# Attention scores written a second time with keys on partitions, in place of transposing the probabilities (16-head ALiBi attention inside a four-layer kernel, one NeuronCore)

## The chip, the cores and the metric

The kernel runs on one core of one Trainium2 chip (trn2). The metric is the device time of one execution in microseconds; 625.41 us is the median of three runs of the kernel before.

## The reference, cut to what matters

Six stages work on a tensor `x` of 1024 tokens by 256 features: a feed-forward stage `ffn0` (dense and 8 experts), a small attention `attn0`, `ffn0` again, `ffn1` (8 experts), the attention `attn1`, and `ffn1` again. Only `attn1` is changed:

```
x = x + _L1_attn_ref(_layernorm(x), ...)          # on (4, 256, 256)

def _L1_attn_ref(hidden_states, w_dkv, w_q, w_uk, w_uv, w_o):
    HEADS = 16; HEAD_DIM = 16; SLOPE = 0.0625
    def alibi_bias(seq_len):                      # i query, j key
        return where(j <= i, -SLOPE * (i - j), -inf)
    c_kv = hidden_states @ w_dkv.T
    q = (hidden_states @ w_q.T).reshape(B, S, HEADS, HEAD_DIM)
    k = (c_kv @ w_uk.T).reshape(B, S, HEADS, HEAD_DIM)
    v = (c_kv @ w_uv.T).reshape(B, S, HEADS, HEAD_DIM)
    scores = einsum("bqhd,bkhd->bhqk", q, k) * HEAD_DIM ** -0.5
    scores = scores + alibi_bias(S)
    attn = softmax(scores, axis=-1)
    out = einsum("bhqk,bkhd->bqhd", attn, v).reshape(B, S, HIDDEN)
    return out @ w_o.T
```

There are 4 samples of 256 tokens and 16 heads, so 64 heads in all, each with a 256 by 256 causal score matrix.

## The kernel before

It is written engine by engine: each engine's program is one list in the order of the code, and semaphores (`wait_ge`, `then_inc`) join them. Nothing is reordered by a scheduler; the order around the change is that of the loops over `hb` below.

`attn1` handles two blocks of 512 tokens (`b` = 0, 1), each of two samples. A block first projects q, the latent and k (every fp32 product as three matmuls of a high and a low part, `split3`, lines 447 to 449), and builds the stacked operands `qs` and `ks` with two 512-column matmuls for each pair of heads (lines 703 and 704). `qs` and `ks` hold 48 rows for a head: three parts of 16, at partitions 0 to 47 for even heads and 64 to 111 for odd ones. They are of type fp32r, `pb`, `pbt` and `va` are plain fp32.

Then comes the head loop, `for hb in range(2 * HEADS)`, 32 heads for each block:

- TensorE, `scores(hd)` (lines 713 and 715): queries on partitions. 128 columns for the first half of the queries (its keys are the first 128), 256 for the second half. The causal quarter that is all masked is never computed. It writes one of three banks.
- VectorE, `bias_min(hd)` (line 1471): adds `bias` (ALiBi and mask) to the negated scores in PSUM and takes each row's minimum into `nmin`, one instruction for 128 columns and one for 256.
- ScalarE, lines 989 and 991: the exponential with `nmin` as its per-partition bias, into `pb`.
- TensorE, `probs_turn(hd - 3)` (line 723): three 128 by 128 transposes of `pb` into another bank, since the next product needs the keys on partitions.
- ScalarE for heads 1 and 3 of four (line 1011) and VectorE for 0 and 2 (line 1479), `probs_t`: copy the result to `pbt`.
- TensorE, `pv` (line 737): for a group of four heads, probabilities times values, with a column of ones in `va` that gives the sum of the row. Its two halves `c` stand in two neighbouring iterations. ScalarE copies the group's result out (`out_t`).
- `out_back`, `out_turn` and `out_project` (lines 754, 761 and 447 to 449) finish a sample's output; they stand at fixed iterations of the loop. `transposes` (line 457) turns the next block's normalised input.

`ffn0` and `ffn1` are long streams of 128-row, 256- and 512-column matmuls.

Of the kernel before, what the change touches and what calls it, by code (L numbers as in the profile page):

```python
# [48 lines left out]
STEP = 64  # L49

# [7 lines left out]
def program(nc, x_in, w0, w1, wr, pre, posts, att0, r0, ident_in, cap_in, iota_in, wa, sel_in, bias_in, out,  # L58
            stages=STAGES):
    with ExitStack() as ctx:  # L60
# [80 lines left out]
        sel = sb("sel", [P, 4, 4, P], F32R)  # L141
        bias = sb("bias", [P, 3 * P])
# [8 lines left out]
        pb = sb("pb", [P, 4, 3 * P])  # L151
        pbt = sb("pbt", [P, 2, 4, 3 * P])

        wa_raw = va[:, :, :, :].rearrange("p t h s -> p (t h s)")[:, 0:WA]
        sel_raw = pbt[:, :, :, :].rearrange("p g j q -> p (g j q)")[:, 0:16 * P]
# [6 lines left out]
        nmin = sb("nmin", [P, 4, 2])  # L162
# [85 lines left out]
        sm_s = sem("scores_biased")  # L248
        exp_s = sem("probs_ready")
        t_ps = sem("probs_t_in_psum")  # L250
        ptd_s = sem("probs_t_by_dve")
        pta_s = sem("probs_t_by_act")
# [47 lines left out]
        by_act = (1, 3)  # L300

        def copied(hd):

            mine = [j for j in range(4) if (j in by_act) == (hd % 4 in by_act)]
            return pta_s if hd % 4 in by_act else ptd_s, len(mine) * (hd // 4) + mine.index(hd % 4) + 1

        def pv_bank(g):

            return 2 if g % 8 == 7 else 5

        def score_bank(hd):
            return hd % (2 * HEADS) % 3

        def turn_bank(hd):
            return (3, 4, 6)[hd % 3]
# [35 lines left out]
        def _(pool):  # L351
# [74 lines left out]
            for st in plan:  # L426
# [10 lines left out]
                if st.kind == "ffn1" and st.k == 0 and "attn1" in stages:  # L437
                    pool.wait_ge(wal_s, WL)
                    nc.gpsimd.memset(va[:, :, :, :], 0.0).then_inc(wal_s, 1)
                    pool.wait_ge(wal_s, WL + 1)  # L440
                    nc.gpsimd.memset(va[:, :, :, HD:HD + 1], 1.0).then_inc(wal_s, 1)


        @block.tensor
        def _(pe):
# [156 lines left out]
            def attn1(st):  # L602
                p = st.p
                for b in range(2):
# [42 lines left out]
                    for hb in range(2 * HEADS):  # L647
                        hd = 2 * HEADS * b + hb
                        if hb == 0:
                            continue  # L650
                        if hb < HEADS:
                            s = HEADS // 2 + hb // 2
                            pe.wait_ge(std_s if s % 2 else sta_s, 8 * b + s // 2 + 1)
                        if hb < 3:
                            pe.wait_ge((sta_s, std_s)[hb - 1], 8 * b + 7)
                        scores(hd)
# [8 lines left out]
                        for i, (at, step) in enumerate(zip((7, 9, 12, 14), 2 * (out_back, out_turn, out_project))):  # L665
                            if hb == HEADS + at:
                                step(2 * b, i // 3)
                    probs_turn(2 * HEADS * (b + 1) - 3)
                    out_turn(2 * b, 1)
                    probs_turn(2 * HEADS * (b + 1) - 2)  # L670
                    for c in range(2):
                        pv(8 * (b + 1) - 2, c)
                    probs_turn(2 * HEADS * (b + 1) - 1)
                    if b == 0 or st.after:

                        transposes(p + b + 1)
                    out_project(2 * b, 1)
                    for c in range(2):
                        pv(8 * (b + 1) - 1, c)
# [27 lines left out]
            def scores(hd):  # L707
# [3 lines left out]
                if hd >= 3:  # L711
                    pe.wait_ge(exp_s, hd - 2)
# [5 lines left out]
            def probs_turn(hd):  # L718
                pe.wait_ge(exp_s, hd + 1)
                if hd >= 3:  # L720
                    pe.wait_ge(*copied(hd - 3))
                for c in range(3):
# [341 lines left out]
        def _(dve):  # L1064
# [325 lines left out]
            def attn1(st):  # L1390
                p = st.p
                for b in range(2):
# [37 lines left out]
                    for hb in range(2 * HEADS):  # L1430
# [7 lines left out]
                        if hb:  # L1438
                            bias_min(hd)
# [193 lines left out]
```

## Time and profile before

| | |
|---|---|
| median of three runs | 625.41 us (622.27 to 628.8) |
| profiled execution: its span | 628.7 us; the page gives the execution no other time, and the highest run was 628.8 |
| TensorE matmul busy | 584.4 us, 93% of the span |
| TensorE weight load busy | 467.3 us, 74% |
| VectorE, ScalarE, GpSimd busy | 433.0, 270.5 and 82.9 us |
| mean granted TensorE clock | 0.883 |

Busy shares are of the whole span. A matmul's end is modelled in the trace, so a matmul is busy longer than the engine needs for it; the distance between the starts of two neighbours tells what one costs. The clock is a share of full speed (2.4 GHz): 1.00 or 0.50, and a mean between them where it changed inside a stretch.

### The profile page before, as it was taken

The page shows a single profiled execution, that of the slowest core. Times are in us where ns is not written, and L with a number is a line of the kernel's source. Part 1 is how long each engine was busy: PE and PEld are TensorE (multiplying, and loading weights), DVE is VectorE, ACT ScalarE, POOL GpSimd, SP SyncE. Part 2 cuts the span into 40 slices and gives each one's busy share as a digit, 9 for nine tenths or more (in the row PEclk, how much of TensorE's full clock was granted, in tenths as well). Part 3 has the DMA queues.
Part 4 walks back from the last instruction along what each step waited for, and adds up shares of the span by engine and source line. Part 5 has one row for each costly group of instructions (what it writes and reads, how often), then busy time and mean ns, then how long its engine had stood idle before and what let it go on. Part 6 is the DMA issues. An engine that isn't in the chain of part 4 may idle for free.

```text
span 628.7 us, 9327 instructions
## 1 busy us (share of the span) xinstructions
PE 584.4 (93%) x3170; PEld 467.3 (74%) x3170; DVE 433.0 (69%) x1251; ACT 270.5 (43%) x603; POOL 82.9 (13%) x94
## 2 busy tenths in 40 slices
PE   2999999999689999999999589899999999999995
PEld 1788888888568888888888578765566855568885
DVE  4667985887853457648778899786454784546986
ACT  3557434632212253245426235264543465443341
POOL 1001000010110000000103536300000000003442
PEclk9999999999869999999999799895556965559998
DMA  5322202000000000000000030000000000000001
GB/s 174 103 93 82 84 19 66 18 2 0 1 1 1 0 1 2 2 0 1 2 0 2 0 139 1 1 1 2 1 1 1 0 2 2 0 1 2 2 33 34
DMA packets 7102, 13.75 MB, mean 22 GB/s; under 512 B 1296, under 2 KB 3600, under 8 KB 6928
## 3 DMA queue, kind: packets, MB, share of 16 engines
q1 hardware_dynamic: 6000, 12.65, 6.3%
q10 hardware_dynamic: 1056, 0.51, 0.3%
q8 instruction: 26, 0.43, 0.3%
q14 instruction: 20, 0.16, 0.1%
HBM read 12.11 MB, written 1.05 MB: 21 GB/s over the span
## 4 chain that ended last, share of the span: by engine, by line
PE 81%; DVE 11%; issue 3%; ACT 2%; POOL 1%; DMA 1%; ACTq 1%; DVEq 0%; POOLq 0%
PE ps L447 19%; PE ps L449 18%; PE ps L448 18%; PE ps L723 8%; PE ps L737 4%; PE ps L713 4%; PE ps L715 3%; DVE gel L1203 3%; PE ps L457 1%; PE ps L703 1%; DVE z L1125 1%; DVE gel L1201 1%; PE ps L704 1%; PE ps L754 1%; DMA post_b<-in_posts_dram 1%
## 5 line engine op out<-in xcount | busy, mean ns | idle before, releaser
L447 PE MATMUL ps<-zh,w0u_h 128*128 128x512 f32 x256 | 102.8, 402 | 2.5 <-issue 2.5
L449 PE MATMUL ps<-zl,w0u_h 128*128 128x512 f32 x256 | 102.2, 399 | 0.0
L448 PE MATMUL ps<-zh,w0u_l 128*128 128x512 f32 x256 | 101.8, 398 | 0.0
L870 ACT ACTIVATE gel<-ps 128x512 f32<-128x512 f32 x64 | 38.2, 597 | 105.5 <-PE ps L449 105.3
L1221 DVE TENSOR_TENSOR act<-gel,ps 128x512 f32<-128x512 f32 x64 | 43.8, 685 | 53.5 <-ACT gel L870 53.4
L447 PE MATMUL ps<-w0d_h,ah 128*128 128x256 f32 x256 | 73.3, 286 | 1.2 <-DVE al L1228 1.0
L448 PE MATMUL ps<-w0d_h,al 128*128 128x256 f32 x256 | 72.4, 283 | 0.0
L449 PE MATMUL ps<-w0d_l,ah 128*128 128x256 f32 x256 | 72.4, 283 | 0.0
L1471 DVE CUSTOM_DVE_ANT_0 ps<-ps,bias 128x128 f32<-128x128 f32 (+1 forms) x128 | 43.2, 383 | 41.0 <-PE ps L715 40.8
L1228 DVE TENSOR_TENSOR al<-act,ah 128x512 fp32r<-128x512 f32 x64 | 43.9, 687 | 23.5 <-ACT ah L876 23.2
L407 POOL TENSOR_TENSOR al<-act,ah 128x512 fp32r<-128x512 f32 x32 | 42.1, 1316 | 137.1 <-ACT ah L944 136.7
L876 ACT ACTIVATE ah<-act 128x512 fp32r<-128x512 f32 x64 | 40.3, 630 | 41.5 <-DVE act L1221 41.5
L447 PEld LDWEIGHTS ps<-zh,w0u_h 128*128 128x128 f32 x256 | 49.0, 191 | 12.1 <-issue 2.9
L449 PEld LDWEIGHTS ps<-zl,w0u_h 128*128 128x128 f32 x256 | 48.8, 191 | 11.8
L448 PEld LDWEIGHTS ps<-zh,w0u_l 128*128 128x128 f32 x256 | 49.0, 192 | 9.3
L723 PE MATMUL ps<-ident,pb 128*128 128x128 f32 x192 | 54.3, 418 | 0.0
L447 PEld LDWEIGHTS ps<-w0d_h,ah 128*128 128x128 f32 x256 | 48.8, 191 | 4.4 <-issue 2.2
L1203 DVE SCALAR_TENSOR_TENSOR gel<-ps,aff,gel 128x256 f32<-128x256 f32 x112 | 46.3, 475 | 7.3 <-PE ps L449 5.9
L448 PEld LDWEIGHTS ps<-w0d_h,al 128*128 128x128 f32 x256 | 48.9, 191 | 2.3
L449 PEld LDWEIGHTS ps<-w0d_l,ah 128*128 128x128 f32 x256 | 49.0, 192 | 0.0
L447 PE MATMUL ps<-w_h,ah 128*128 128x256 f32 x128 | 37.9, 296 | 11.6 <-DVE gel L1201 7.4
L1203 DVE SCALAR_TENSOR_TENSOR macc<-ps,aff,macc 128x256 f32<-128x256 f32 x112 | 46.3, 476 | 0.7 <-PE ps L449 0.2
(180 smaller groups left out, 1156.1 us busy)
## 6 DMA issues: line engine op xcount, KB each, us to landing
stage<-in_w_dram SPq DMA_DIRECT2D x16, 384.0 KB, 3.0
stage<-in_w_dram SPq DMA_DIRECT2D x8, 256.0 KB, 2.6
x<-in_x_dram SPq DMA_DIRECT2D x2, 512.0 KB, 5.1
pbt<-in_sel_dram SPq DMA_DIRECT2D x1, 1024.0 KB, 6.6
out_dram<-x SPq DMA_DIRECT2D x2, 512.0 KB, 2.9
va<-in_wa_dram SPq DMA_DIRECT2D x1, 896.0 KB, 5.1
post_b<-in_posts_dram ACTq DMA_DIRECT2D x1, 388.0 KB, 5.6
bias<-in_bias_dram SPq DMA_DIRECT2D x1, 192.0 KB, 7.2
```

The lines of the kernel that those rows point to most:

```text
L407: nc.gpsimd.tensor_tensor(al[:, slot, :], act32[:, n % 2, :], ah[:, slot, :].bitcast(F32), ALU.subtract).then_inc(al1_s, 1)
L447: pe.matmul(o, lh, rh, start=start, stop=False, **kw)
L448: pe.matmul(o, ll, rh, start=False, stop=False, **kw)
L449: return pe.matmul(o, lh, rl, start=False, stop=stop, **kw)
L713: pe.matmul(ps[:, score_bank(hd), 0:P], qs[r0:r1, h // 2, t0:t0 + P], ks[r0:r1, h // 2, t0:t0 + P], start=True, stop=True)
L723: mm = pe.transpose(ps[:, turn_bank(hd), c * P:(c + 1) * P], pb[:, hd % 4, c * P:(c + 1) * P], ident[:, :])
L870: nc.scalar.activation(gel[:, n % 2, :], ps[:, 2 * (n % 2), :], ACT.Gelu_apprx_tanh).then_inc(gelu_s, 1)
L876: nc.scalar.activation(ah[:, n % NA, :], act32[:, n % 2, :], ACT.Copy).then_inc(ah_s, 1)
L1203: i = V.scalar_tensor_tensor(sums[:, t, :], o, a, sums[:, t, :], ALU.mult, ALU.add)
L1221: V.tensor_tensor(act32[:, n % 2, :], gel[:, n % 2, :], ps[:, 2 * (n % 2) + 1, :], ALU.mult)\
L1228: V.tensor_tensor(al[:, n % NA, :], act32[:, n % 2, :], ah[:, n % NA, :].bitcast(F32), ALU.subtract)\
L1471: i = V.tensor_tensor_reduce(s, s, bias[:, lo:hi], 1.0, FAR, ALU.add, ALU.min, nmin[:, hd % 4, c:c + 1])
```

## The change

The scores are computed twice. The first time (queries on partitions) they serve only for the row minimum. The minima of four heads are then split into a high and a low part and written, with constants, as columns of the tile `shift`; TensorE transposes `shift` once for four heads (`shift_turn`) and ScalarE copies it to `shift_t`. The second time (`scores_t`, keys on partitions) four matmuls add into one bank: the row minimum and the ALiBi term from `shift_t` (33 rows, 384 columns), the scores of the two halves (48 rows, 128 and 256 columns), and the causal mask (128 rows, 256 columns). The exponential reads that bank and writes `pbt` at once, so `pb`, the transposes of probabilities and the copies to `pbt` are gone. `scores_t` runs 6 iterations behind `scores`, and the loop has 12 iterations more (`SUM`) in which no new head starts. `bias` now lies in `tmp` and `shift` in `macc`; the constants `sel` grow by half.

```diff
-        sel = sb("sel", [P, 4, 4, P], F32R)
+        sel = sb("sel", [P, 6, 4, P], F32R)
...
         def score_bank(hd):
-            return hd % (2 * HEADS) % 3
-        def turn_bank(hd):
-            return (3, 4, 6)[hd % 3]
+            return hd % 2
+        def turned_bank(hd):
+            return 3 + hd % 2
...
# TensorE, head loop
-                    for hb in range(2 * HEADS):
+                    for hb in range(2 * HEADS + SUM):
...
-                        scores(hd)
...
-                        if hb >= 3:
-                            probs_turn(hd - 3)
-                        if hb % 4 in (1, 2) and hb >= 8:
-                            pv(hd // 4 - 2, hb % 4 - 1)
...
+                        if 0 < hb < 2 * HEADS:
+                            scores(hd)
...
+                        if hb % GROUP == 1 and GROUP < hb < 2 * HEADS + GROUP:
+                            shift_turn(hd // GROUP - 1)
+                        if TURN <= hb < 2 * HEADS + TURN:
+                            scores_t(hd - TURN)
+                        if hb % GROUP == 0 and hb >= SUM:
+                            for c in range(2):
+                                pv((hd - SUM) // GROUP, c)
...
-            def probs_turn(hd):
-                pe.wait_ge(exp_s, hd + 1)
-                if hd >= 3:
-                    pe.wait_ge(*copied(hd - 3))
-                for c in range(3):
-                    mm = pe.transpose(ps[:, turn_bank(hd), c * P:(c + 1) * P], pb[:, hd % 4, c * P:(c + 1) * P],
-                                      ident[:, :])
-                mm.then_inc(t_ps, 1)
+            def shift_turn(g):
+                if g == 0:
+                    pe.wait_ge(shz_s, 2)
+                pe.wait_ge(shl_s, g + 1)
+                if g:
+                    pe.wait_ge(sht_s, g)
+                for i, block in enumerate((3, 0, 2)):
+                    mm = pe.transpose(ps[:, 2, i * P:(i + 1) * P], shift[:, g % 2, block, :], ident[:, :])
+                mm.then_inc(sht_ps, 1)
+
+            def scores_t(hd):
...
+                pe.wait_ge(sht_s, hd // GROUP + 1)
+                if hd >= 2:
+                    pe.wait_ge(exp_s, hd - 1)
+                pe.matmul(ps[:, bank, 0:3 * P], sel[r0:r0 + LATE_ROW + 1, 4, hd % GROUP, :],
+                          shift_t[r0:r0 + LATE_ROW + 1, hd // GROUP % 2, :], start=True, stop=False,
+                          skip_group_check=True)
+                pe.matmul(ps[:, bank, 0:P], ks[r0:r1, h // 2, t0 + P:t0 + 2 * P], qs[r0:r1, h // 2, t0 + P:t0 + 2 * P],
+                          start=False, stop=False, skip_group_check=True)
+                pe.matmul(ps[:, bank, P:3 * P], ks[r0:r1, h // 2, t0:t0 + P], qs[r0:r1, h // 2, t0:t0 + 2 * P],
+                          start=False, stop=False, skip_group_check=True)
+                pe.matmul(ps[:, bank, 0:2 * P], sel[:, 5, 0, :], sel[:, 5, 1:3, :].rearrange("p c q -> p (c q)"),
+                          start=False, stop=True, skip_group_check=True).then_inc(t_ps, 1)
...
# ScalarE
-                        nc.scalar.activation(pb[:, hd % 4, 0:P], ps[:, score_bank(hd), 0:P], ACT.Exp,
-                                             bias=nmin[:, hd % 4, 0:1], scale=-1.0)
-                        nc.scalar.activation(pb[:, hd % 4, P:3 * P], ps[:, score_bank(hd), P:3 * P], ACT.Exp,
-                                             bias=nmin[:, hd % 4, 1:2], scale=-1.0).then_inc(exp_s, 1)
...
+            def shift_out(g):
+                act.wait_ge(sht_ps, g + 1)
+                if g >= 2:
+                    act.wait_ge(t_ps, GROUP * (g - 1))
+                nc.scalar.activation(shift_t[:, g % 2, :], ps[:, 2, 0:3 * P], ACT.Copy).then_inc(sht_s, 1)
...
-                nc.scalar.activation(pbt[:, hd // 4 % 2, hd % 4, :], ps[:, turn_bank(hd), 0:3 * P], ACT.Copy)\
-                  .then_inc(pta_s, 1)
+                nc.scalar.activation(pbt[:, hd // GROUP % 2, hd % GROUP, :], ps[:, turned_bank(hd), 0:3 * P], ACT.Exp,
+                                     scale=-1.0).then_inc(exp_s, 1)
...
# VectorE
-            def probs_t(hd):
...
-                V.tensor_copy(pbt[:, hd // 4 % 2, hd % 4, :], ps[:, turn_bank(hd), 0:3 * P]).then_inc(ptd_s, 1)
+            def shift_hi(g):
...
+                V.tensor_copy(hi.bitcast(F32R), m).then_inc(shh_s, 1)
+
+            def shift_lo(g):
+                m, hi, lo = shifts(g)
+                dve.wait_ge(shh_s, g + 1)
+                V.tensor_tensor(lo, m, hi, ALU.subtract).then_inc(shl_s, 1)
```

TensorE before, in the middle of the head loop of the first block: `L713` and `L715` are the scores of one head, `L723` the transposes of the head three before it, `L737` half of a group's product with the values (its stationary operand has 32 columns; shapes are stationary columns by moving columns).

```order
L713 MATMUL ps<-ks,qs 128x128
L715 MATMUL ps<-ks,qs 128x256
L723 MATMUL ps<-ident,pb 128x128 x3
L737 MATMUL ps<-pbt,va 32x256 x4
L713 MATMUL ps<-ks,qs 128x128
L715 MATMUL ps<-ks,qs 128x256
L723 MATMUL ps<-ident,pb 128x128 x3
L737 MATMUL ps<-pbt,va 32x128 x4
```

TensorE in the changed kernel at the same place, with its own line numbers: `L715` and `L717` are the scores, `L738` to `L745` the four matmuls of `scores_t`, `L757` the product with the values, `L727` the transposes of `shift`.

```order
L715 MATMUL ps<-ks,qs 128x128
L717 MATMUL ps<-ks,qs 128x256
L738 MATMUL ps<-shift_t,sel 128x384
L741 MATMUL ps<-qs,ks 128x128
L743 MATMUL ps<-qs,ks 128x256
L745 MATMUL ps<-sel 128x256
L757 MATMUL ps<-pbt,va 32x256 x4
L757 MATMUL ps<-pbt,va 32x128 x4
L715 MATMUL ps<-ks,qs 128x128
L717 MATMUL ps<-ks,qs 128x256
L727 MATMUL ps<-ident,macc 128x128 x3
L738 MATMUL ps<-shift_t,sel 128x384
```

Three transposes of each head gave way to four matmuls of each head, three transposes stand once in four heads, and the two halves of the product with the values now follow each other.

ScalarE before, in the same loop: two exponentials for each head and, for every second one, the copy of line 1011.

```order
L989 ACTIVATE pb<-ps,nmin 128x128
L991 ACTIVATE pb<-ps,nmin 128x256
L1011 ACTIVATE pbt<-ps 128x384
L989 ACTIVATE pb<-ps,nmin 128x128
L991 ACTIVATE pb<-ps,nmin 128x256
```

ScalarE in the changed kernel: `L1028` is the exponential of a head, `L1022` the copy to `shift_t`, `L1035` the copy of a group's output.

```order
L1028 ACTIVATE pbt<-ps 128x384 x3
L1022 ACTIVATE shift_t<-ps 128x384
L1028 ACTIVATE pbt<-ps 128x384
L1035 ACTIVATE gel<-ps 128x256
L1028 ACTIVATE pbt<-ps 128x384 x3
```

One instruction of 384 columns for a head took the place of two exponentials and half a copy.

## Rows read from the trace of the kernel before

**Rows 1.** The page's chain of work that ended last, its shares by line

```profile
PE ps L447 19%; PE ps L449 18%; PE ps L448 18%; PE ps L723 8%; PE ps L737 4%; PE ps L713 4%; PE ps L715 3%; DVE gel L1203 3%; PE ps L457 1%; PE ps L703 1%; DVE z L1125 1%; DVE gel L1201 1%; PE ps L704 1%; PE ps L754 1%; DMA post_b<-in_posts_dram 1%
```

**Rows 2.** Windows: busy of PE, PEld, DVE, ACT, POOL, clock, DMA

```profile
410.00:416.00 6.00, 6.00 (x32) 4.86 (x31) 5.72 (x12) 3.98 (x7) 0.00 (x0) 1.00 0.01 3
422.00:428.00 6.00, 6.00 (x23) 3.87 (x23) 5.43 (x29) 3.65 (x11) 0.61 (x2) 0.58 0.00 0
464.00:470.00 6.00, 6.00 (x29) 4.10 (x28) 3.37 (x15) 3.28 (x9) 0.00 (x0) 0.50 0.00 0
476.00:482.00 6.00, 6.00 (x40) 4.47 (x40) 2.38 (x8) 1.92 (x5) 0.00 (x0) 0.58 0.00 0
482.00:488.00 6.00, 4.96 (x43) 3.95 (x43) 3.31 (x8) 2.37 (x7) 0.00 (x0) 1.00 0.01 3
```

**Rows 3.** Timeline of PE, four heads (start, busy, line, shapes)

```profile
442.24 0.47 PE L713 MATMUL ps<-ks,qs 48*128 48x128 f32 x1
442.51 0.52 PE L715 MATMUL ps<-ks,qs 48*128 48x256 f32 x1
442.96 0.90 PE L723 MATMUL ps<-ident,pb 128*128 128x128 f32 x3
443.79 0.47 PE L713 MATMUL ps<-ks,qs 48*128 48x128 f32 x1
...
445.35 1.08 PE L737 MATMUL ps<-pbt,va 128*32 128x256 f32 x8
446.36 0.47 PE L713 MATMUL ps<-ks,qs 48*128 48x128 f32 x1
...
447.91 0.66 PE L737 MATMUL ps<-pbt,va 128*32 128x128 f32 x8
448.50 0.47 PE L713 MATMUL ps<-ks,qs 48*128 48x128 f32 x1
...
450.05 0.47 PE L713 MATMUL ps<-ks,qs 48*128 48x128 f32 x1
```

**Rows 4.** Timeline of PE, one head of the second block, before the clock fell

```profile
506.35 0.33 PE L713 MATMUL ps<-ks,qs 48*128 48x128 f32 x1
...
506.77 0.55 PE L723 MATMUL ps<-ident,pb 128*128 128x128 f32 x3
507.25 0.32 PE L713 MATMUL ps<-ks,qs 48*128 48x128 f32 x1
```

**Rows 5.** Timeline of PE, the end of an output projection inside the loop

```profile
469.43 0.41 PE L448 MATMUL ps<-wa_h,otl 128*128 128x256 f32 x1
469.64 0.41 PE L449 MATMUL ps<-wa_l,oth 128*128 128x256 f32 x1
469.99 0.47 PE L713 MATMUL ps<-ks,qs 48*128 48x128 f32 x1
```

**Rows 6.** Timeline of PE, both halves of a group's product with the values

```profile
479.00 1.50 PE L737 MATMUL ps<-pbt,va 128*32 128x256 f32 x16
480.44 0.79 PE L723 MATMUL ps<-ident,pb 128*128 128x128 f32 x3
```

**Rows 7.** Timeline of DVE, the start of one head's minimum and of the next

```profile
420.45 0.33 DVE L1471 CUSTOM_DVE_ANT_0 ps<-ps,bias 128x128 f32<-128x128 f32 x1
...
421.08 0.33 DVE L1471 CUSTOM_DVE_ANT_0 ps<-ps,bias 128x128 f32<-128x128 f32 x1
```

**Rows 8.** Groups of ACT, 428 to 476 us (busy, mean ns, idle before)

```profile
L991 ACT ACTIVATE pb<-ps,nmin 128x256 f32<-128x256 f32 x24 | 11.2, 467 | 0.0
L989 ACT ACTIVATE pb<-ps,nmin 128x128 f32<-128x128 f32 x24 | 8.8, 368 | 24.0 <-DVE nmin L1471 24.0
L1011 ACT ACTIVATE pbt<-ps 128x384 f32<-128x384 f32 x12 | 5.9, 488 | 0.0
L1018 ACT ACTIVATE gel<-ps 128x256 f32<-128x256 f32 x4 | 1.5, 384 | 0.0
```

**Rows 9.** Timeline of PE, head 6 of the first block

```profile
423.51 0.47 PE L713 MATMUL ps<-ks,qs 48*128 48x128 f32 x1
```

**Rows 10.** Timeline of PE, the last output transposes, the second block's first matmul

```profile
484.87 1.09 PE L754 MATMUL ps<-ident,act 128*128 128x128 f32 x8 [0.50 <-ACT act L1018]
485.72 0.48 PE L447 MATMUL ps<-zh,wa_h 128*128 128x512 f32 x1
```

More of the change, by code:

```diff
@@ L49 @@
 STEP = 64
+GROUP = 4
+ONE_ROW, LATE_ROW = 2 * GROUP, 32
+TURN = 6
+SUM = 12
+OUT_STEPS = (27, 29, 32, 34, 36, 38)
 Stage = namedtuple("Stage", "s kind p k before after d0 d1")
@@ L140, in program @@
         wa_l = sb("wa_l", [P, WA], F32R)
-        sel = sb("sel", [P, 4, 4, P], F32R)
-        bias = sb("bias", [P, 3 * P])
+        sel = sb("sel", [P, 6, 4, P], F32R)
+        bias = tmp[:, :, :].rearrange("p t d -> p (t d)")[:, 0:3 * P]
         ch = sb("ch", [P, BLK], F32R)
@@ L298, in program @@
         TK = 11
[L300 to L305, printed above, removed]
         def pv_bank(g):
-            return 2 if g % 8 == 7 else 5
+            return 6 if g % 8 == 7 else 5
         def score_bank(hd):
-            return hd % (2 * HEADS) % 3
-        def turn_bank(hd):
-            return (3, 4, 6)[hd % 3]
+            return hd % 2
+        def turned_bank(hd):
+            return 3 + hd % 2
         def out_bank(n, t):
@@ L441, in _ @@
                     nc.gpsimd.memset(va[:, :, :, HD:HD + 1], 1.0).then_inc(wal_s, 1)
+                    nc.gpsimd.memset(shift[:, :, :, :], 0.0).then_inc(shz_s, 1)
+                    pool.wait_ge(shz_s, 1)
+                    for r in range(2):
+                        c = STEP * r
+                        nc.gpsimd.memset(shift[:, :, :, c + ONE_ROW:c + ONE_ROW + 1], 1.0)
+                        i = nc.gpsimd.memset(shift[:, :, 3, c + LATE_ROW:c + LATE_ROW + 1], 1.0)
+                    i.then_inc(shz_s, 1)
         @block.tensor
@@ L660, in attn1 @@
                             pe.wait_ge(v_s, b + 1)
-                        if hb >= 3:
-                            probs_turn(hd - 3)
-                        if hb % 4 in (1, 2) and hb >= 8:
-                            pv(hd // 4 - 2, hb % 4 - 1)
[L665 to L679, printed above, removed]
+                        if hb % GROUP == 1 and GROUP < hb < 2 * HEADS + GROUP:
[5 more added lines that the diff above has]
+                                pv((hd - SUM) // GROUP, c)
+                        if hb in OUT_STEPS:
+                            i = OUT_STEPS.index(hb)
+                            (out_back, out_turn, out_project)[i % 3](2 * b, i // 3)
+                        if hb == 2 * HEADS + 1 and (b == 0 or st.after):
+                            pe.wait_ge(sm_s, 2 * HEADS * (b + 1))
+                            transposes(p + b + 1)
                 if st.after != "ffn1":
@@ L730, in pv @@
                 if c == 0:
-                    for j in (2, 3):
-                        pe.wait_ge(*copied(4 * g + j))
+                    pe.wait_ge(exp_s, GROUP * (g + 1))
                     if g and pv_bank(g) == 5:
@@ L1615 @@
                         sel[(2 * pair + e) * HD + r, kind, pair, STEP * e + HD * part + r] = 1.0
+    for r in (0, STEP):
+        for j in range(GROUP):
+            sel[r + j, 4, j, :] = sel[r + GROUP + j, 4, j, :] = -1.0
+            sel[r + ONE_ROW, 4, j, :] = -0.0625 * np.arange(P)
+            sel[r + LATE_ROW, 4, j, :] = -0.0625 * P
+    sel[:, 5, 0, :] = np.eye(P)
+    sel[:, 5, 1, :] = sel[:, 5, 2, :] = np.where(np.arange(P)[:, None] > np.arange(P)[None, :], FAR, 0.0)
     q, j = np.arange(SEQ)[:, None], np.arange(SEQ)[None, :]
-    far = np.where(j <= q, 0.0625 * (q - j), FAR).astype(np.float32)
+    far = np.where(j <= q, -0.0625 * j, FAR).astype(np.float32)
     bias = np.concatenate([far[:P, :P], far[P:, :]], axis=1)
```

117 lines of the change are left out of this document (62 added, 55 removed).

## The prediction

> **What bounds the kernel now.** I read first the page's chain of work that ended last. It lies almost wholly on TensorE, most of it in the feed-forward streams (lines 447 to 449), which the change leaves alone; the head loop of the attention (lines 723, 737, 713 and 715) makes up 19% of the span [rows 1]. So the question is what the change does to TensorE's time in the two head loops, and little else.
>
> Then I read the windows. In the head loop TensorE is busy 6.00 of every 6 us, VectorE and ScalarE about half of that [rows 2]: the loop is bound by TensorE alone. The same rows show that the granted clock is 1.00 (2.4 GHz) while 512-column matmuls on 128 rows run, mixes both levels in the window from 422 us, is 0.50 (1.2 GHz) at 464, and comes back inside 476 to 482. The reader is to see that a TensorE that is busy all the time runs most of this loop at half speed. Two things set the time of this change: how much the engine has to stream and to switch, and at which of the two clocks.
>
> Third, the timeline gives the cost of each piece, from start to start, at 1.2 GHz [rows 3]. Scores of a head: 442.24 to 442.96, 0.72 us. Three transposes: 442.96 to 443.79, 0.83 us. Together 1.55 us for a head. The product with the values adds 446.36 - 445.35 = 1.01 us for one half and 448.50 - 447.91 = 0.59 us for the other, and a group of four heads takes 450.05 - 442.24 = 7.81 us. At 2.4 GHz the scores take 0.42 us and the transposes 0.48 [rows 4].
>
> **Prices for the new pieces.** Inside a run of 256-column matmuls on 128 rows, 469.43 to 469.64 gives 0.21 us, or 0.83 ns a column [rows 5]. The 384 columns of scores are then 0.32 us of streaming, and 0.72 - 0.32 = 0.40 us goes to changing to 48 rows and back out of them. Three transposes at the same 0.21 us are 0.64, and 0.19 us is switching. One such pair of switches costs 0.59 us at 1.2 GHz. That is the largest hidden cost here, as the new order keeps the switches: the scores and the first three matmuls of scores_t run on 48 or 33 rows, then the mask matmul runs on 128 rows, and then the next head begins.
>
> **Part by part, at 1.2 GHz.**
>
> - Removed: three transposes for each head, 0.64 us of streaming. Their 0.19 us of switching, and the 0.40 us of the scores, are inherited by the mask matmul and by the run ahead of it.
> - Added: scores_t, 384 + 128 + 256 + 256 = 1024 columns, 0.85 us of streaming, and a pair of switches. No row shows fp32r matmuls going from 48 to 128 rows. The cheapest row is 128 to 48 rows, 469.64 to 469.99, 0.35 us for a matmul of 0.21, so 0.14 for a change and 0.28 for two [rows 5]. The dearest reading is that every short matmul on few rows pays what line 713 pays, 0.27 us for 0.11 of streaming, 0.16 more, three times over in scores_t: 0.59 + 0.48 = 1.07. I take 0.53, next to the 0.59 which the same places cost now and a little under it, since the mask matmul loads fp32r, not fp32. scores_t is 1.38 us.
> - Added: shift_turn once in four heads. It breaks the run of few-row matmuls in two, so it costs a full transposing part and one more entry: 0.83 + 0.40 = 1.23 us.
> - Moved: the two halves of the product with the values now stand together; where they do so already, they take 480.44 - 479.00 = 1.44 us [rows 6] against 1.01 + 0.59 = 1.60. This gives back 0.16 us a group.
> - ScalarE: one exponential of 384 columns. Between 128 and 256 columns it grows by 0.10 us, so 0.57, and with a quarter of a 0.49 us copy and of a 0.38 us copy 0.79 us a head [rows 8]. VectorE: its minimum takes 0.63 us a head as now [rows 7], and two small instructions for four heads stand in place of two copies. Both engines stay well under TensorE's head, so I cost what they save at nothing; TensorE's own work covers it.
> - New waits: scores_t waits for the exponential of the head two before it, because of its bank, and scores for the minimum two before. Each has one whole head of TensorE's work, over 1.5 us, against 0.57 and 0.63. shift_turn stands 2 iterations behind the minimum that it needs, the first use of shift_t one iteration behind shift_turn. Covered in the loop; behind shift_turn everything of TensorE is queued, but it would wait only in the first group, where TensorE has little else to do.
> - The larger constants, the clearing of shift and the moved bias lie beside the feed-forward streams: nothing.
>
> **The sum for one block.** In the kernel before, head 6 starts at 423.51 [rows 9] and the next block's first matmul at 485.72 [rows 10]: 62.2 us. My prices reproduce this: 26 heads' scores at 0.32 (8.3), 29 heads of transposes and switches at 1.23 (35.7), products with the values 12.0, output steps 24 matmuls and transposes at 0.21 (5.1), waits 1.0, sum 62.1.
>
> For the changed kernel the scores of the first six heads come at VectorE's pace, 0.63 us each, so scores_t of head 0 begins at about the same 423.5. From there: 32 scores_t at 1.38 (44.2), 25 heads' scores at 0.32 (8.0), 7 shift_turn at 1.23 (8.6), 8 products at 1.44 (11.5), output steps 5.1, the next block's 8 transposes 1.3, waits 1.0: 79.7 us. That is 17.5 us more a block, 35 for both. Against the profiled execution's 628.7 us this is 664; against the median of 625.4, which lies 3.3 lower, **660 us**.
>
> The bounds of scores_t's switching move this: 0.28 in place of 0.53 takes 0.25 x 64 = 16 us off (644), 1.07 adds 0.54 x 64 = 35 us (695). I think the low one nearer, since the second matmul of a run may load its weights behind the one before it.
>
> **Which clock.** The whole sum rests on 1.2 GHz. For it: before the fall at the loop's entry the engine ran scores on 48 rows and a few transposes with waits between them, and the new loop starts thinner still, with nothing but scores at VectorE's pace and three transposes. While the clock is low, the loop before gets through six 256-column matmuls of an output projection on 128 rows, and the clock is still 0.50 in that window [rows 2, 5]. The new loop alternates short matmuls on 48 and 33 rows, one on 128 rows and about a third of the time in switches. It is denser than the old one, but far from the streams that run at 1.00.
>
> **The rivals.**
>
> - The clock comes up and stays up (2.4 GHz through both loops). For it: transposes go, real matmuls take their place, and the clock is the one thing which could change by a factor of two. The price, all with halved streaming: scores_t 0.425 + 0.26 + 0.16 = 0.85 us (the switches from the 0.42 and 0.48 us of [rows 4]), times 32 is 27.0; scores 25 x 0.16 = 4.0; shift_turn 7 x 0.74 = 5.2; products 8 x 0.72 = 5.8; the rest 4.4; 46.4 us a block against 62.2, 32 us less for both: 593 us. This is the case on the other side; it decides when over half of each loop runs at 2.4 GHz, since a block gains 16 us at one clock and loses 17.5 at the other. Against it: the entry, as above. The clock did rise inside 476 to 482, where the engine ran almost only transposes and products with the values, and was 1.00 in the next window [rows 2], so a loop of transposes is not what alone holds it down. I give 10%.
> - The Trainium skill's page "TensorE: Matmul & The Clock Gate", in "Part 4: PE-mode transpose", says that the full clock doesn't engage for transposes, as these don't count as TensorE being busy in the same way; by that rule taking out transposes for matmuls would free the clock, and the time would be that of this first rival. The trace speaks against it at 476 to 482.
> - The clock comes up for part of the loops, about half: gain and loss cancel, about 624 us. 6%.
> - The few-row matmuls hide no load at all, or the wait for shift_t shows in each group: above 684 us. 3%.
>
> **How the numbers follow.** The forecast, low clock and prices within the bounds, has 81%. Its range, 640 to 684 us, takes in the lower bound and two thirds of the way to the upper one; the rest, the two cases of a higher clock and the heavy tail, is 19% and left out. About 1%, 6 us, is what a measurement of this kernel can tell from no change. Faster by more: the first rival and some of the second, 14%. Within 1%: 4%. Slower: 82%.
>
> **What would show it.** In the profile after: the granted clock of the windows from 425 to 495 us, 0.50 by the forecast and 1.00 by the rival; the distance from one head's scores to the next, 1.7 us (four heads with their group's work 9.5 against 7.81), or 1.0 at 2.4 GHz; TensorE's idle time in the loops still near nothing, with ScalarE at under half; the feed-forward stages unchanged to a microsecond. I am wrong if the clock is high, wrong in size if the mask matmul's switches differ from 0.53 us, and wrong in kind if TensorE waits for ScalarE or VectorE in the middle of the loop.

## The result and the profile after

The changed kernel takes 688.8 us (median of 4 runs, 685.2 to 692.5), the kernel before 627.0 us (622.3 to 628.8) in the same job: 1.104 times as long, 95% interval 1.094 to 1.113. I had forecast 660 us with a range up to 684. The sign and the mechanism came out, the size didn't: +60.3 us between the profiled spans (689.0 against 628.7), where my working gave +35. A few executions keep or lose the full clock over a whole loop (of the kernel before, two took 598.6 and 598.9 us at a mean clock of 0.947 and two 699.9 and 702.5 us at 0.71, the others 618.6 to 631.0 at 0.88 to 0.91), so where the runs of an experiment split like this, each kind is given.

The first view is again the page, with its slices of the granted clock and its chain of work that ended last.

```profile
PEclk9999999998599999999989997555559555557998
...
PE ps L456 18%; PE ps L458 17%; PE ps L457 17%; PE ps L745 5%; PE ps L738 4%; PE ps L757 3%; PE ps L715 3%; PE ps L743 3%; PE ps L717 3%; DVE gel L1220 2%; PE ps L727 2%; PE ps L466 2%; PE ps L705 1%; PE ps L774 1%; DVE z L1142 1%
```

The chain is the one of [rows 1] with the head loop's lines exchanged: 745, 738, 757, 715, 743, 717 and 727 make up 23% of 689 us, where 723, 737, 713 and 715 made up 19% of 629. The two long stretches of 5 in the clock's line are the head loops. In the samples of the clock they last 92.2 us from 421.8 and 95.6 us from 534.5; before, 58.0 from 423.0 and 54.6 from 508.3. So the level in the loops, 0.50, is as forecast, and the slow stretches grew by 34 and 41 us.

The windows (columns as in [rows 2]), in the middle of the loop, at its end and where the next block begins:

```profile
464.00:470.00 6.00, 6.00 (x25) 4.27 (x27) 2.60 (x14) 1.62 (x4) 0.00 (x0) 0.50 0.00 0
506.00:512.00 6.00, 4.22 (x26) 2.59 (x25) 1.93 (x4) 1.07 (x4) 0.00 (x0) 0.50 0.00 0
512.00:518.00 6.00, 5.59 (x28) 4.70 (x29) 2.84 (x8) 1.97 (x5) 0.00 (x0) 0.83 0.00 0
```

In the middle TensorE (second column) has work in all of the 6 us, VectorE in 2.60 and ScalarE in 1.62: the loop is still bound by TensorE alone. What is new against [rows 2] stands at the end: before, the clock came up inside 476 to 482, ahead of the loop's tail; now it stays at 0.50 to the end of the tail and comes up at 514.0, as the next block's streams begin (after the second block at 630.1, 2.8 us into them).

The timeline of TensorE, one head in the middle of the loop, its successor's first row, and a head before which `shift_turn` stands; it answers to [rows 3]:

```profile
442.31 0.47 PE L715 MATMUL ps<-ks,qs 48*128 48x128 f32 x1
442.58 0.52 PE L717 MATMUL ps<-ks,qs 48*128 48x256 f32 x1
442.90 0.52 PE L738 MATMUL ps<-shift_t,sel 33*128 33x384 f32 x1
443.22 0.30 PE L741 MATMUL ps<-qs,ks 48*128 48x128 f32 x1
443.33 0.52 PE L743 MATMUL ps<-qs,ks 48*128 48x256 f32 x1
443.77 0.58 PE L745 MATMUL ps<-sel 128*128 128x256 f32 x1
444.29 0.47 PE L715 MATMUL ps<-ks,qs 48*128 48x128 f32 x1
...
449.95 0.52 PE L717 MATMUL ps<-ks,qs 48*128 48x256 f32 x1
450.41 0.90 PE L727 MATMUL ps<-ident,macc 128*128 128x128 f32 x3
...
453.07 0.52 PE L717 MATMUL ps<-ks,qs 48*128 48x256 f32 x1
```

A head takes 444.29 - 442.31 = **1.98 us**, against 1.55 before and a forecast of 1.70. The price of each matmul is the distance between its start and the next one's, less the streaming at 0.83 ns a column. Line 738, 384 columns, takes 443.22 - 442.90 = 0.32 us: all streaming. Line 741, 0.11 us: all streaming. But 743 to 745, where the rows go from 48 to 128, is 0.44 us for 0.21 of streaming; 745 to the next head's 715, back to 48 rows, 0.52 for 0.21 (0.31 more); 715 itself takes 0.27 for 0.11, and 717 takes 0.32 for 0.21. Of the 1.98 us, 1408 columns stream for 1.17, and 0.81 us is switching, where I had allowed 0.53. The kernel before has 0.59 of it in the same places [rows 3]: its way out of the 48 rows (0.45 for 0.21) and its first load (0.27 for 0.11) cost what they cost here, its way back behind three transposes only 0.19, and it has no third load in the run, the one that costs 0.11 here.

The weight loads (PEld) of the same head show why the dear places are the ones after a change:

```profile
442.30 0.28 PEld L715 LDWEIGHTS ps<-ks,qs 48*128 48x128 f32 x1 [0.22 <-issue]
442.47 0.33 PEld L717 LDWEIGHTS ps<-ks,qs 48*128 48x128 f32 x1
442.69 0.33 PEld L738 LDWEIGHTS ps<-shift_t,sel 33*128 33x128 f32 x1
442.90 0.33 PEld L741 LDWEIGHTS ps<-qs,ks 48*128 48x128 f32 x1
443.22 0.33 PEld L743 LDWEIGHTS ps<-qs,ks 48*128 48x128 f32 x1
443.77 0.29 PEld L745 LDWEIGHTS ps<-sel 128*128 128x128 f32 x1 [0.22 <-issue]
```

Four loads follow each other at about 0.2 us from 442.30, no faster, and the short matmuls at the start of the run go at their pace; from line 741 on the load starts a whole matmul ahead of its own (442.90 for 443.22). At 443.77 and 442.30 the load engine stood still for 0.22 us and the load starts together with its matmul. Such a load isn't hidden behind an earlier matmul.

The end of the block, which answers to [rows 5] and [rows 10]. The rows at 500.37 and 501.93 are the starts of two `scores_t` with no new scores between them, 1.56 us apart:

```profile
495.75 0.58 PE L745 MATMUL ps<-sel 128*128 128x256 f32 x1
496.13 1.91 PE L466 MATMUL ps<-ident,z 128*128 128x128 f32 x8
...
500.37 0.69 PE L738 MATMUL ps<-shift_t,sel 33*128 33x384 f32 x1
...
501.93 0.69 PE L738 MATMUL ps<-shift_t,sel 33*128 33x384 f32 x1
...
508.84 0.55 PE L456 MATMUL ps<-wa_h,oth 128*128 128x256 f32 x1 [1.68 <-DVE otl L1526]
...
512.40 1.84 PE L774 MATMUL ps<-ident,act 128*128 128x128 f32 x8 [0.50 <-ACT act L1035]
514.01 0.48 PE L456 MATMUL ps<-zh,wa_h 128*128 128x512 f32 x1
```

The groups of ScalarE in the loop, 428 to 488 us (busy, mean ns, idle before), against [rows 8]:

```profile
L1028 ACT ACTIVATE pbt<-ps 128x384 f32<-128x384 f32 x23 | 11.3, 491 | 31.6 <-PE ps L745 31.6
L1022 ACT ACTIVATE shift_t<-ps 128x384 fp32r<-128x384 f32 x6 | 2.9, 491 | 13.6 <-PE ps L727 13.6
```

Both of ScalarE's groups wait for TensorE, 45.2 of 60 us. The exponential of 384 columns takes 0.49 us, less than the 0.57 I had estimated, and that changes nothing.

### The profile page after: what moved, and what is told of

It is laid out like the page before. It is cut to its first block, busy times and chain, and to the rows that moved or that the text cites. A ratio compares the mean times of both kernels' runs of the same rounds, so it can differ in the third digit from the quotient of the medians.

```text
span 689.0 us, 9401 instructions
## 1 busy us (share of the span) xinstructions
PE 640.9 (93%) x3282; PEld 519.3 (75%) x3282; DVE 425.2 (62%) x1251; ACT 251.0 (36%) x523; POOL 84.1 (12%) x99
## 4 chain that ended last, share of the span: by engine, by line
PE 83%; DVE 10%; issue 3%; ACT 1%; POOL 1%; DMA 1%; ACTq 1%; DVEq 0%; POOLq 0%
PE ps L456 18%; PE ps L458 17%; PE ps L457 17%; PE ps L745 5%; PE ps L738 4%; PE ps L757 3%; PE ps L715 3%; PE ps L743 3%; PE ps L717 3%; DVE gel L1220 2%; PE ps L727 2%; PE ps L466 2%; PE ps L705 1%; PE ps L774 1%; DVE z L1142 1%
## 5 line engine op out<-in xcount | busy, mean ns | idle before, releaser
L1488 DVE CUSTOM_DVE_ANT_0 ps<-ps,tmp 128x128 f32<-128x128 f32 (+1 forms) x128 | 43.3, 383 | 82.1 <-PE ps L717 82.0
L1028 ACT ACTIVATE pbt<-ps 128x384 f32<-128x384 f32 x64 | 31.4, 491 | 91.5 <-PE ps L745 91.5
```

Of the source, the lines that this page charges most:

```text
L1028: nc.scalar.activation(pbt[:, hd // GROUP % 2, hd % GROUP, :], ps[:, turned_bank(hd), 0:3 * P], ACT.Exp, scale=-1.0).then_inc(exp_s, 1)
L1488: i = V.tensor_tensor_reduce(s, s, bias[:, lo:hi], 1.0, FAR, ALU.add, ALU.min, nmin[:, hd // GROUP % 2, c, hd % GROUP:hd % GROUP + 1])
```

## The experiments

Three questions were open: is the extra time the price of changing rows (theory A in the expectations), would the new loop be cheap at the full clock and could it be brought there (theory C), and is it a load's place in the run or the step from 48 to 33 rows that costs 0.11 us at line 717. Each edit is made to the changed kernel, unless the kernel before is named. "Filler" is a matmul whose result nothing uses: it writes a score bank that the scores then overwrite.

Whole times compare these kernels only roughly, since the clock changes its level at different places near the ends of their loops. In the profiled executions, from a block's first `scores_t` to the next stage's first matmul, it is 1.00 for none of the changed kernel's 90.8 + 90.8 us, for 0.1 us without the mask matmul, but for 14.4 us with the mask on 48 rows, 8.9 with the mask on VectorE and 11.7 with the masks in pairs. At 0.50 such a stretch would last up to twice as long. So I also give the time of a group of four heads in the middle of the first loop, where all of them run at 0.50: 10.49 us in the changed kernel.

### The mask matmul on the head's own 48 rows

```diff
-                pe.matmul(ps[:, bank, 0:2 * P], sel[:, 5, 0, :], sel[:, 5, 1:3, :]...
+                pe.matmul(ps[:, bank, 0:2 * P], sel[r0:r1, 5, 0, :], sel[r0:r1, 5, 1:3, :]...
```

> The changed kernel with the mask matmul (256 columns) on the same 48 rows as the scores, in place of 128 rows; the mask is then complete for 48 of 128 keys only. Columns are the same, the change between 48 and 128 rows goes from each head. Theory A (the loss is largely the cost of changing between 48 and 128 rows, at 1.2 GHz): a head falls from 1.98 us to about 1.5, 64 heads give back 27 to 32 us, about 658 us. Rival B (it is the added columns alone): nothing moves, 687 to 690 us. The clock stays at 0.50 in either.

Measured 637.3 us (636.4 to 637.8), 1.018 of the kernel before (1.010 to 1.026), 51.5 us less than the changed kernel with the same columns streamed. Up to 14 us of that can be the clock at the ends of the loops. In the middle, at 0.50, a group falls from 10.49 to 6.87 us, 0.90 us a head, more than the 0.54 of switching on the two sides of the mask matmul, and more than all 0.81 of a head. The timeline of TensorE shows where the rest comes from:

```profile
441.19 0.52 PE L717 MATMUL ps<-ks,qs 48*128 48x256 f32 x1
...
442.47 0.69 PE L738 MATMUL ps<-shift_t,sel 33*128 33x384 f32 x1
442.49 0.47 PE L715 MATMUL ps<-ks,qs 48*128 48x128 f32 x1
442.76 0.52 PE L717 MATMUL ps<-ks,qs 48*128 48x256 f32 x1
442.96 0.30 PE L741 MATMUL ps<-qs,ks 48*128 48x128 f32 x1
443.07 0.52 PE L743 MATMUL ps<-qs,ks 48*128 48x256 f32 x1
...
448.06 0.52 PE L717 MATMUL ps<-ks,qs 48*128 48x256 f32 x1
```

Line 738 starts at 442.47 and the next head's 715 at 442.49, though 738 alone streams for 0.32 us. An even head lies on rows 0 to 47, an odd one on 64 to 111, and matmuls of the two run beside each other. The second head even runs ahead of the program: in TensorE's list its 715 and 717 stand behind the first head's 741 and 743, and they start before these. A group of four heads takes 448.06 - 441.19 = 6.87 us from line 717 to line 717, where the changed kernel takes 453.07 - 442.58 = 10.49 and the kernel before 7.81. The one matmul on 128 rows for each head costs its two changes, and besides it fences the heads off from one another. (A group now costs less than in the kernel before, and the kernel is still slower: the two stretches from the first `scores_t` to the next stage take 60.9 and 66.3 us, those of the kernel before, from head 6 on, 62.2 and 61.0. What the middle gains goes to the longer end of the loop.)

### No mask matmul

Its three lines are left out (and the matmul before it ends the accumulation). The mask is then missing, and the exponential's scale is -0.01, so that values stay finite.

> The changed kernel without the mask matmul: the causal mask is left out of the second scores, and the exponential takes them times 0.01 so that nothing overflows. Theory A: the head loses 0.21 us of streaming and its changes of rows, 1.98 to about 1.25 us, 64 heads give back 45 us, about 643 us. Rival B (columns alone): 0.21 x 64 = 14 us back, 675 us.

Measured 632.6 us (628.6 to 636.8), 1.011 (1.001 to 1.021), 56.2 us back with the clock at 0.50 to the end of both loops. Streaming the mask's columns accounts for 64 x 0.21 = 14 us of it at most, so 42 us or more are its rows. In the middle of the loop, from one group's product with the values to the next, it is 447.07 - 440.62 = 6.45 us, 0.42 less than with the mask on 48 rows, though 4 x 0.21 us of columns are gone. Against the 3.6 us a group that moving it to 48 rows gave, what costs is the rows of that matmul, hardly its columns.

### The mask added by VectorE

```diff
-                pe.matmul(ps[:, bank, 0:2 * P], sel[:, 5, 0, :], sel[:, 5, 1:3, :]...
...
+            def mask_add(hd):
+                dve.wait_ge(t_ps, hd + 1)
+                s = ps[:, turned_bank(hd), 0:2 * P]
+                V.tensor_tensor(s, s, sel[:, 5, 1:3, :].rearrange("p c q -> p (c q)").bitcast(F32), ALU.add).then_inc(msk_s, 1)
```

The exponential waits for `msk_s` in place of `t_ps`.

> The changed kernel with the causal mask added by VectorE into the bank of the second scores ahead of the exponential, in place of the mask matmul; all of the reference is computed. Theory A (TensorE's changes to 128 rows and back were the price): TensorE as in the run without the mask, VectorE takes 0.45 us more for a head beside it, 632 to 640 us. Rival E (VectorE's step in the chain becomes the wait): TensorE idles in the loop, 650 us or more.

Measured 639.0 us (636.4 to 641.8): 49.8 us back (up to 9 of them the clock at the loops' ends), with all of the computation kept, as theory A wanted. A group takes 447.21 - 439.99 = 7.22 us. TensorE now waits now and then for the longer chain behind it:

```profile
445.24 0.65 PE L739 MATMUL ps<-shift_t,sel 33*128 33x384 f32 x1 [0.49 <-ACT pbt L1027]
```

VectorE's addition of 256 columns takes 0.44 us a head; in the window 440 to 446 TensorE is busy for 5.51 us at clock 0.50. Even so this version is some 13 us behind the kernel before.

### The masks of two heads together

```diff
+                            if hb % 2:
+                                mask(hd - TURN - 1)
+                                mask(hd - TURN)
...
-                pe.matmul(ps[:, bank, 0:3 * P], sel[r0:r0 + LATE_ROW + 1, 4, hd % GROUP, :],
+                pe.matmul(ps[:, bank, 0:3 * P], sel[r0:r1, 4, hd % GROUP, :],
```

This halves the changes of rows and keeps every column on TensorE; the product with the values moves one head back. The shift's matmul takes 48 rows in place of 33 too.

> The changed kernel in another order, all of the reference computed: the few-row matmuls of two heads run first and then their two mask matmuls one after the other, the product with the values stands behind them, and the first matmul of the second scores reads 48 rows in place of 33 (the added ones are zero). Theory A (each change to 128 rows and back costs 0.70 us at 1.2 GHz beyond streaming): half of the changes go, 0.35 us or more for each head, 22 to 32 us, 657 to 667 us; more if neighbouring heads, on other rows of the array, run beside each other as they did in the run with the 48-row mask. Theory A2 (the 0.11 us that the 33-row matmul waits for behind the 48-row one is due to the change of rows): that distance falls from 0.32 to 0.21 us. Rival B (columns alone): 687 us.

Measured 656.3 us (653.9 to 661.5), 1.052 (1.044 to 1.061): 32.5 us back, at the upper end of theory A's 22 to 32, which it let grow if heads ran beside each other; up to 12 of it can be the clock at the loops' ends. A group takes 444.74 - 436.68 = 8.06 us. The other half of the edit changes nothing:

```profile
440.60 0.47 PE L718 MATMUL ps<-ks,qs 48*128 48x128 f32 x1
440.87 0.52 PE L720 MATMUL ps<-ks,qs 48*128 48x256 f32 x1
441.13 0.47 PE L718 MATMUL ps<-ks,qs 48*128 48x128 f32 x1
441.19 0.59 PE L741 MATMUL ps<-shift_t,sel 48*128 48x384 f32 x1
```

From line 720 to 741 it is 0.32 us, as from 717 to 738 in the changed kernel, with 48 rows in place of 33. That speaks against the step from 48 to 33 rows as what costs 0.11 us there, and for the place in the run, the third load after a change. It isn't a clean test, as a matmul on the other rows now starts in between (718 at 441.13).

### Fillers in the changed kernel

```diff
+                pe.matmul(ps[:, score_bank(hd), :], wa_h[:, 0:P], wa_h[:, 0:4 * P], start=True, stop=True)
```

One filler of 512 columns on 128 rows ahead of each head's scores. The question is the rival of the full clock.

> The changed kernel with one extra 512-column matmul on 128 rows ahead of each head's first scores, into the bank that these then overwrite; its result is not used. Theory C (the clock at 1.2 GHz holds this loop back, and denser work on 128 rows keeps it at 2.4): clock 1.00 in most of the loops, a head about 1.3 us, 30 us less for each block, 615 to 635 us. Rival D (the clock doesn't answer to such work here): 0.43 us more for each head, 715 to 722 us.

Measured 707.5 us (704.8 to 711.7), 1.132 (1.123 to 1.142), with the clock at 0.50 in both loops. A head takes 445.82 - 443.41 = 2.41 us, 0.43 more. Theory C failed, and the rival was right that in the loop the filler is only added; the whole is 8 us under its 715 to 722. Next, four fillers for each of heads 1 to 5 and one for each later head:

> The changed kernel with the 128-row filler, four of them for each of heads 1 to 5 of a block, where nothing but scores runs, and one for each later head. Theory C (the clock was lost in the thin stretch at the entry, and the filled loop would hold 2.4 GHz if it came in with it): clock 1.00 through both loops, a head about 1.3 us, a block 54 us against 62 before, 605 to 620 us. Rival D (this loop can't hold the clock even so): clock 0.50, 708 to 715 us.

Measured 704.1 us (695.7 to 707.3), within 4 us of the run before and over 80 us above theory C. The clock held through the entry, until 433.6 us, and fell there, where one filler a head was left: 0.97 in the window 428 to 434, 0.50 in 440 to 446. Then two fillers for each later head, and two in each of a block's last six `scores_t`:

> The changed kernel with two 128-row fillers for each head (four for heads 1 to 5 of a block), and two for each of the last six heads' second scores. Theory C: enough to hold 1.00 through both loops; a head with its fillers takes about 1.6 us, 0.46 to 0.5 us of it the fillers, so both blocks together 35 to 50 us less than the changed kernel, 640 to 655 us. Without the fillers a head would take 1.1 us at this clock. Rival D: the clock still falls, 0.86 us more for each head, 740 us.

Measured 684.2 us (three runs 683.1 to 685.5, one 655.8 with a mean clock of 0.969). The profiled execution has both levels, the first block's loop at one and the second's at the other:

```profile
440.00:500.00 60.00, 60.00 (x217) 38.94 (x217) 14.59 (x78) 11.39 (x25) 0.00 (x0) 0.50 0.00 1
548.00:612.00 64.00, 64.00 (x389) 42.94 (x387) 28.83 (x152) 20.31 (x45) 1.20 (x2) 1.00 0.01 1
```

```profile
560.11 0.33 PE L717 MATMUL ps<-ks,qs 48*128 48x128 f32 x1
...
561.17 0.63 PE L716 MATMUL ps<-wa_h 128*128 128x512 f32 x2
561.73 0.32 PE L717 MATMUL ps<-ks,qs 48*128 48x128 f32 x1
```

The timeline shows a head of the second block. With two fillers it takes 561.73 - 560.11 = 1.62 us; less the fillers' 1024 columns, 0.43 us at 2.4 GHz, that leaves 1.19 us. (The same working at 0.50 in this run, 448.93 - 446.10 = 2.83 less 0.85, gives 1.98, the head of the changed kernel.) The kernel before takes 0.90 at that clock [rows 4], so the new form gives TensorE more to do at either clock. My rival of 593 us had 0.85 + 0.16 = 1.01 us in its place: its price was 0.18 us a head too low, and its condition didn't come. Both expectations of this run missed: the three runs at 683 to 685 us have the mean clock of the profiled one, 0.92 to 0.93, with one block high and one low.

The last of them is the version with the mask on VectorE, with four fillers at the entry, two or one later:

> The version with the mask added by VectorE, with fillers on 128 rows: four for heads 1 to 5 of a block, two for two heads of each group of four, one for the others, two for each of the last six heads' second scores. All of the reference is computed. Theory C: clock 1.00 in both loops, then VectorE (1.1 us a head) and TensorE (1.1 to 1.3) are about level, 590 to 610 us, faster than both kernels. Rival: the clock falls, 670 us.

Measured 707.3 us (704.5 to 708.7), 1.132 (1.124 to 1.140), with the clock at 0.50 for 75.1 us from 427.8 and for 81.9 from 547.2. The expectation failed by a hundred microseconds. Fillers that don't hold the clock are only columns, and beside that they fence the heads off again.

### Fillers in the kernel before

The same line of 512 columns, put ahead of the scores in the kernel before:

> The kernel before with the same extra 512-column matmul ahead of each head's scores, result not used. Theory C: clock 1.00 in the head loops, a head about 1.15 us in place of 1.55, 15 us less for each block, about 595 us, faster than both kernels. Rival D: clock stays 0.50, 0.43 us more for each head, about 655 us.

Measured **598.7 us** (596.3 to 601.5), 0.958 of the kernel before (0.949 to 0.966). The window in the middle of the loop has the clock at 1.00, and so has the whole attention; [rows 2] have 0.50 at 464:

```profile
440.00:446.00 6.00, 6.00 (x45) 3.71 (x44) 3.91 (x20) 3.96 (x11) 0.00 (x0) 1.00 0.00 0
```

```profile
440.11 0.32 PE L714 MATMUL ps<-ks,qs 48*128 48x128 f32 x1
...
440.53 0.55 PE L724 MATMUL ps<-ident,pb 128*128 128x128 f32 x3
440.83 0.47 PE L713 MATMUL ps<-wa_h 128*128 128x512 f32 x1
441.24 0.32 PE L714 MATMUL ps<-ks,qs 48*128 48x128 f32 x1
```

A head with its filler takes 441.24 - 440.11 = 1.13 us, where without it and at 0.50 it was 1.55 [rows 3]. All the transposes are still there. The same 512 columns on the head's 48 rows (`wa_h[r0:r1, 0:P], wa_h[r0:r1, 0:4 * P]`):

> The kernel before with the same 512-column filler for each head, but on the 48 rows of the head's own scores in place of 128; result not used. It streams the same columns and changes rows no more often than without it. Theory C1 (the clock follows how long the array streams, whatever the rows): clock 1.00 as with the 128-row filler, 596 to 602 us. Theory C2 (rows in use count too): the clock falls at the loop's entry and stays at 0.50 in the loops, 0.43 us more for each head than before, 650 to 660 us.

Three runs at 650.6 to 654.7 us and one at 626.0 (mean clock 0.918, against 0.87), and in the profiled one the clock is at 0.50 in both loops:

```profile
440.00:446.00 6.00, 6.00 (x26) 3.99 (x26) 2.51 (x11) 3.29 (x9) 0.00 (x0) 0.50 0.00 0
```

TensorE is as busy by the profile in both, with the same columns. On 128 rows they held the clock in all four executions, on 48 rows in three of four they didn't. With 256 columns on 128 rows:

> The kernel before with a filler of 256 columns in place of 512, on 128 rows. Theory C: still enough to hold the clock at 1.00, 0.10 us less for each head than the 512-column filler, about 592 us. Rival: too thin, the clock falls to 0.50 in the loops and the filler costs 0.21 us a head on top of the kernel before, about 640 us.

Measured 616.1 us (613.1 to 622.9), between the two: in the profiled execution the first loop is at 0.50 (68.3 us of it), the second at 1.00 from end to end. Last, 512 columns for the first eight heads of a block and 256 for the others:

> The kernel before with the 128-row filler of 512 columns for the first eight heads of a block and of 256 columns for the other 24, results not used. The kernel with 256 columns everywhere lost the clock at the entry of one block and held it at 1.00 through the whole other one. Theory F (the entry decides, and 256 columns hold the clock once the loop runs): clock 1.00 in both blocks in every execution, 0.10 us less for each of 48 heads than with 512 columns, 592 to 595 us. Rival G (the loop with 256 columns also loses it in the middle): a block at 0.50 costs about 24 us, 610 to 620 us.

Five runs at 592.2 to 596.1 us, one at 627.3 with a mean clock of 0.912. In the profiled execution the clock is 1.00 in both loops, and a head takes 431.45 - 430.43 = 1.02 us:

```profile
430.43 0.32 PE L715 MATMUL ps<-ks,qs 48*128 48x128 f32 x1
...
431.45 0.32 PE L715 MATMUL ps<-ks,qs 48*128 48x128 f32 x1
```

That is 30 us less than the 626.2 of the kernel before in that job, for most executions, and the fastest version here; the form with 512 columns throughout is the steadier of the two in these few runs.

## Why the prediction was wrong in size

- **The bound and the clock: right.** TensorE is busy for 6.00 of 6 us in the loop at 0.50, ScalarE and VectorE wait for it. That TensorE would wait for ScalarE or VectorE in the middle of the loop didn't happen.
- **The step that failed is the term "I take 0.53" for the switching of `scores_t`.** Stretches of nothing but `scores_t` have 1.56 us a head (500.37 to 501.93) where I had 1.38, so the term is 0.71. I had started from 0.59, what the same places cost in the kernel before, and gone a little under it because the mask matmul loads fp32r. No run shows anything to take off for that. And one of the places got dearer: the way out to 128 rows costs 0.23 and the first load 0.17, as before, but the way back from the one mask matmul costs 0.30, where behind three transposes it cost 0.19. Of this 0.30, 0.17 is paid too where transposes on 128 rows come next (495.75 to 496.13, 0.38 us for 0.21), so it belongs to the mask matmul's standing alone and not to the rows behind it. The rest is the 0.14 us of my lower bound [rows 5], the way back to 48 rows when a long stream on 128 rows stands before it.
- **A second term: the scores at 0.32 us a head.** I had given all switching of the run to `scores_t`, but head by head the scores add 1.98 - 1.56 = 0.42 us: one more load among those that follow each other at the start of a run. With the first term this makes 0.53 into the 0.81 us of a head.
- **The range.** The time lay within my bounds for the switching (0.28 to 1.07, 644 to 695 us), but I stopped the range two thirds of the way up without a row that said so. What I had above 684 us, 3%, was tied to loads never hidden or to a wait for `shift_t`, and neither came: from the fourth on the loads are hidden.
- **Right within 0.1 us:** `shift_turn` costs (453.07 - 449.95) - 1.98 = 1.14 us against 1.23 forecast, and the joined product with the values 1.44 as forecast. Together: four heads at 0.18 + 0.10 more, less 0.10, make 9.47 into 10.5; measured 10.49.
- **The block.** From the first `scores_t` (423.20) to the next block's first matmul is 90.8 us against my 79.7. Of the missing 11.1, 32 x 0.18 = 5.8 are `scores_t`, 25 x 0.10 = 2.5 the scores, and -0.7 `shift_turn`. The waits at the end are 1.68 + 0.50 in place of 1.0, and the eight transposes at line 466 take 1.83 in place of 1.3, which is 1.7 more. The last 1.8 I can't assign row by row. The second block takes 90.8 us too (536.46 to 627.28), where the kernel before took 62.2 and 61.0: 58.4 of the 60.3 us lie in these two stretches.
- **What caused it is shown, not only argued.** Taking the changes of rows out takes a group of four heads at the same low clock from 10.49 to 6.87 us (mask on 48 rows), 6.45 (no mask) and 7.22 (mask on VectorE), and taking half of them out to 8.06; the whole times fall by 51.5, 56.2, 49.8 and 32.5 us.
- **It is also more than a sum of switches.** With the mask matmul on few rows, heads on different rows run beside each other, which I had not thought of. The trace of the kernel before shows it in one place, where no transposes stand between the scores of two heads (x2: one row for two matmuls that start together):

```profile
419.15 0.33 PE L713 MATMUL ps<-ks,qs 48*128 48x128 f32 x2
419.31 0.34 PE L715 MATMUL ps<-ks,qs 48*128 48x256 f32 x2
```

- **A row that I said was missing.** I wrote that no row shows fp32r matmuls going from 48 to 128 rows. One does, at the full clock: 0.26 us for 0.11 of streaming, 0.15 more for the way out alone, which spoke for the dearer side.

```profile
416.85 0.33 PE L715 MATMUL ps<-ks,qs 48*128 48x256 f32 x1
417.11 0.50 PE L703 MATMUL ps<-ah,sel 128*128 128x512 f32 x1
```

- **The rival of the full clock** didn't come. Had it come for the new loop alone, a head at 1.19 us would have beaten the 1.55 of the kernel before; with the clock high in both, 1.19 stands against 0.90. One filler didn't lift it here, and the change lengthened the stretch at 1.2 GHz. The Trainium skill ("TensorE: Matmul & The Clock Gate", "Part 4: PE-mode transpose") says that the full clock doesn't engage for transposes. The runs here don't follow the number of transposes: the kernel before with fillers runs at 1.00 for all of the attention with all its three transposes a head, and the changed loop, with few transposes, runs at 0.50.

What stays open is what exactly holds the clock. The runs show that 512 useless columns a head on 128 rows do in the one loop and not in the other, and on 48 rows mostly not; a rule is not to be had from them.

## What to carry to other kernels

Price a matmul by what stands before and behind it: one matmul on 128 rows among matmuls on 48 cost 0.5 us of switching at 1.2 GHz beside 0.21 of streaming, and stopped heads on separate rows from overlapping. Put such work together, on the same rows, or on an engine that idles (here VectorE, 50 us back). When a loop is bound by TensorE, read the granted clock first: where it was 0.50 on a busy engine, a line of useless 128-row work took 28 us off the kernel before. But it has to be tried: in the changed loop the same line cost 19.

## What the runs showed of the hardware

- Matmuls on rows 0 to 47 and on 64 to 111 run beside each other if nothing on 128 rows stands between them, and those of the later head start ahead of matmuls that stand before them in the program: starts 442.47 and 442.49, group of four 6.87 in place of 10.49 us.
- Useless work can speed a kernel up: 627 to 599 us, with the clock at 1.00 where it had been 0.50. The same columns on 48 rows made it slower (650.6) in three of four executions.
- Loads of short matmuls after a change of rows follow each other at 0.17 to 0.22 us at 1.2 GHz; from the fourth on they are hidden.
- A change between 48 and 128 rows costs, at 1.2 GHz and beyond streaming, 0.23 us on the way out and 0.30 on the way back behind a single matmul of 256 columns.
